# Loads, batches and splits in the setup of a four-layer kernel: the scan's weights first, up to four blocks per PSUM bank

## The reference

```
x = x + scan_attention(layernorm(x))    # attn_W, freq_W, out_W, proj_W, identity; 9 doubling steps
x = x + experts(layernorm(x))           # dense gated MLP + top-8 of 1024 experts by product keys
x = x + linear_attention(layernorm(x))  # Wq, Wk, Wv, Wo, gamma, beta
x = x + experts(layernorm(x))           # the same weights as the second layer
```

## Time and profile before

| | us |
|---|---|
| median of 3 runs | 2409.92 (2403.93 to 2412.46) |
| profiled execution | 2408.92 |
| its span | 2407.2 |
| PE busy | 2224.7 (92%) |
| DVE busy | 1902.4 (79%) |
| ACT busy | 1127.6 (47%) |
| POOL busy | 80.9 (3%) |
| mean granted clock of PE | 0.987 |

### The profile page before, as it was taken

One profiled execution on the slowest core, in us unless ns is written; L12 is line 12 of the kernel. 1 busy time (PEld: TensorE's weight loads), 2 busy tenths in 40 slices (PEclk: granted clock), 3 DMA queues, 4 the chain that ended last, 5 costly groups with the idle time before them and its releaser, 6 DMA issues. The chain is left out here.

```text
span 2407.2 us, 37844 instructions
## 1 busy us (share of the span) xinstructions
PE 2224.7 (92%) x12582; PEld 1548.4 (64%) x12582; DVE 1902.4 (79%) x5516; ACT 1127.6 (47%) x1542; POOL 80.9 (3%) x135
## 2 busy tenths in 40 slices
PE   5999999899999999999979999988999999999998
PEld 4777777676576676676734455446576576675674
DVE  5768686689889898998965566556888889898997
ACT  1445454453543544434426666663543544444533
POOL 3200000000000000000000000000000000000000
PEclk9999999999999999999989999999999999999999
DMA  7000000000000000000000000000000000000000
GB/s 210 1 1 0 0 0 1 1 1 1 0 0 0 0 0 0 0 0 0 1 1 1 1 1 0 1 1 1 1 9 9 0 9 9 0 9 9 0 10 9
DMA packets 20761, 18.10 MB, mean 8 GB/s; under 512 B 6555, under 2 KB 19871, under 8 KB 20648
## 3 DMA queue, kind: packets, MB, share of 16 engines
q1 hardware_dynamic: 16106, 14.04, 1.9%
q10 hardware_dynamic: 4542, 2.78, 0.4%
HBM read 12.60 MB, written 4.19 MB: 7 GB/s over the span
## 5 line engine op out<-in xcount | busy, mean ns | idle before, releaser
L1380 ACT ACTIVATE f_E<-f_two 128x1024 f32<-128x1024 f32 x256 | 248.2, 1021 | 324.8 <-PE f_two L1265 324.8
L1111 DVE SCALAR_TENSOR_TENSOR f_E<-f_two,f_E 128x1024 f32<-128x1024 f32 x256 | 311.2, 1221 | 91.1 <-ACT f_E L1380 84.7
L1255 PE MATMUL f_acc<-ue,f_mid 128*128 128x256 f32 x1024 | 251.9, 392 | 6.2 <-DVE f_mid L1096 6.2
L1255 PEld LDWEIGHTS f_acc<-ue,f_mid 128*128 128x128 f32 x1024 | 191.0, 193 | 47.4 <-issue 15.4
L1163 PE MATMUL f_two<-f_hT,wg 128*128 128x512 f32 x768 | 210.3, 409 | 0.0
L1350 ACT ACTIVATE f_gate<-f_two,bg 128x512 f32<-128x512 f32 x128 | 88.1, 688 | 257.6 <-PE f_two L1163 257.3
L1163 PE MATMUL f_two<-f_hT,wu 128*128 128x512 f32 x768 | 199.9, 395 | 0.0
L1835 ACT ACTIVATE b_U<-b_two 128x768 f32<-128x768 f32 (+1 forms) x192 | 158.8, 882 | 65.5 <-PE b_two L1700 64.8
L1163 PE MATMUL f_two<-f_hT,deT 128*128 128x512 f32 x768 | 184.3, 395 | 0.0
L1591 DVE TENSOR_TENSOR b_U<-b_U,tri 128x512 f32<-128x512 f32 x128 | 85.4, 689 | 116.3 <-ACT b_U L1835 116.3
L1163 PEld LDWEIGHTS f_two<-f_hT,wu 128*128 128x128 f32 x768 | 144.2, 188 | 35.0
(11 more groups left out here) (262 smaller groups left out, 3950.7 us busy)
## 6 DMA issues: line engine op xcount, KB each, us to landing
x<-in_L_attn_a_x SPq DMA_DIRECT2D x8, 512.0 KB, 7.5
out_x<-x SPq DMA_DIRECT2D x8, 512.0 KB, 2.9
de_rows<-in_L_ffn_down_embed ACTq DMA_DIRECT2D x1, 1024.0 KB, 6.0
wd<-in_L_ffn_Wd SPq DMA_DIRECT2D x1, 1024.0 KB, 10.1
ue<-in_L_ffn_up_embed SPq DMA_DIRECT2D x16, 64.0 KB, 5.2
whole_g<-in_L_ffn_Wg SPq DMA_DIRECT2D x1, 1024.0 KB, 5.4
whole_u<-in_L_ffn_Wu SPq DMA_DIRECT2D x1, 1024.0 KB, 8.7
ffq<-in_L_ffn_Wq ACTq DMA_DIRECT2D x4, 128.0 KB, 8.9
```

What stands on the lines that cost most here:

```text
L1111: dve.scalar_tensor_tensor(out=two_heads, in0=wide(turns, ("R", u))[:], scalar=PICKED_ABOVE, in1=two_heads, op0=ALU.is_gt, op1=ALU.mult).t ...
L1255: mm = pe.matmul(acc[:, j * C:(j + 1) * C], mixed[c % 2][:, j * P:(j + 1) * P], w.ue[:, c, :], start=False, stop=True, skip_group_check=True)
L1380: act.activation(E[:, c % 2, 2 * p:2 * p + 2].rearrange("p h t -> p (h t)"), wide(turns, ("S", u))[:], ACT.Exp).then_inc(S.act_read, 1)
```

## The change

The nine scan loads are issued ahead of x(0) and x(1). ACT issues its ten loads only when all nine scan loads have landed. SP issues x(2) and all later loads only when ACT's loads and the columns have landed.

A job now holds a list of pieces, each a turn or a product, side by side in one bank: up to four transposes of 128 columns, or four products of 64. TensorE signals after the last piece, and VectorE copies the whole bank with one instruction. The number of transposes and products is as before. The scan's jobs become 4 turns and 12 products, keys and ffq 3 jobs, wsim 4, de 4, wrow 6.

VectorE takes the statistics and moments of x(0) ahead of jobs 6 and 7 and those of x(1) ahead of jobs 8 and 9, and normalises four tiles behind the second wsim job and four behind the fourth. The third subtraction (second half of `deT`) moves from GpSimd to the end of VectorE's list.

```diff
@@ -176,55 +176,59 @@
 
         jobs = []
 
-        def turned(src, dst):
-            jobs.append(([(src, None)], P, dst, 1.0))
+        def turned(srcs, dst):
+            jobs.append(([[(src, None)] for src in srcs], P, dst, 1.0))
+
+        def product(pairs, m, dst, scale):
+            jobs.append(([pairs], m, dst, scale))
 
         for k in range(KC):
-            turned(outw[:, k * P:(k + 1) * P], outwT[:, k, :])
-            for r in range(KC):
-                turned(attnw[:, r, k * P:(k + 1) * P], attnqT[:, k, r * P:(r + 1) * P])
+            cols = slice(k * P, (k + 1) * P)
+            turned([outw[:, cols]], outwT[:, k, :])
+            turned([attnw[:, r, cols] for r in range(KC)], attnqT[:, k, :])
 
         for half in range(2):
...
         scan_jobs = len(jobs)
+        turned([keys[:, k, :] for k in range(KC)], keysT[:])
         for k in range(KC):
-            turned(keys[:, k, :], keysT[:, k, :])
-            for h in range(H):
-                turned(ffq[:, k, h].rearrange("p q n -> p (q n)"), ffqT[:, h, k * P:(k + 1) * P])
-        for q in range(2):
-            for h in range(H):
+            turned([ffq[:, k, h].rearrange("p q n -> p (q n)") for h in range(H)], ffqT[:, :, k * P:(k + 1) * P])
+        for k in range(KC):
+            for q in range(2):
                 rows = slice(q * NKEYS, (q + 1) * NKEYS)
-                for k in range(KC):
-                    jobs.append(([(ffqT[rows, h, k * P:(k + 1) * P],
-                                   keysT[rows, h // 2, (h % 2) * NKEYS:(h % 2 + 1) * NKEYS])],
-                                 P, wsim[:, k, (q * H + h) * NKEYS:(q * H + h + 1) * NKEYS], 1.0))
+                jobs.append(([[(ffqT[rows, h, k * P:(k + 1) * P],
+                                keysT[rows, h // 2, (h % 2) * NKEYS:(h % 2 + 1) * NKEYS])] for h in range(H)],
+                             P, wsim[:, k, q * C:(q + 1) * C], 1.0))
         wsim_made = len(jobs)
         deT_made = []
         for k in range(KC):
-            for e in range(FC):
-                block = deT[:, k].rearrange("p (q i l) -> p i q l", q=LQ, l=NHI)[:, 2 * e:2 * e + 2]
-                turned(de[:, e, k * P:(k + 1) * P], block)
+            for e in range(0, FC, 4):
+                block = deT[:, k].rearrange("p (q i l) -> p i q l", q=LQ, l=NHI)[:, 2 * e:2 * e + 8]
+                turned([de[:, e + n, k * P:(k + 1) * P] for n in range(4)], block)
             deT_made.append(len(jobs))
         for k in range(KC):
-            for r in range(2):
-                turned(wrow[:, 0, r, k * P:(k + 1) * P], w.wqk[:, k, r * P:(r + 1) * P])
-                turned(wrow[:, 1, r, k * P:(k + 1) * P], w.wqk[:, k, C + r * P:C + (r + 1) * P])
-                turned(wrow[:, 2, r, k * P:(k + 1) * P], w.wvb[:, k, r * P:(r + 1) * P])
-                turned(wrow[:, 3, r, k * P:(k + 1) * P], w.wo[:, k, r * P:(r + 1) * P])
+            cols = slice(k * P, (k + 1) * P)
+            turned([wrow[:, m, r, cols] for m in range(2) for r in range(2)], w.wqk[:, k, :])
+            turned([wrow[:, 2, r, cols] for r in range(2)], w.wvb[:, k, :])
+            turned([wrow[:, 3, r, cols] for r in range(2)], w.wo[:, k, :])
+
+        def job_bank(n, pieces, m):
+
+            width = P if pieces[0][0][1] is None else pieces[0][0][1].shape[-1]
+            return bank[n % 4][0:m, 0:width * len(pieces)], width
+
         splits = [(w.wsim[:, 0], w.wsim[:, 1], wsim, wsim_made)]
         for k in range(KC):
             splits.append((w.deT[:, 0, k], w.deT[:, 1, k], deT[:, k], deT_made[k]))
@@ -241,16 +245,17 @@
                     sp.dma_start(w.x[:, b * TJ:(b + 1) * TJ, :],
                                  io.x[b].rearrange("(j p) c -> p j c", p=P)).then_inc(w.x_loaded[b], 16)
 
+                for dst, src in scan_loads:
+                    sp.dma_start(dst, src, allow_slow_non_contiguous=True).then_inc(scan_loaded, 16)
                 load_x(0)
                 load_x(1)
-                for dst, src in scan_loads:
-                    sp.dma_start(dst, src, allow_slow_non_contiguous=True).then_inc(scan_loaded, 16)
                 for signal in w.all_signals:
                     sp.sem_inc(signal, START)
                 sp.sem_inc(signals_open, 1)
                 sp.wait_ge(features_cleared, 1)
                 for dst, src in columns:
                     sp.dma_start(dst, src, allow_slow_non_contiguous=True).then_inc(loaded, 16)
+                sp.wait_ge(loaded, 16 * (len(loads) + len(columns)))
                 for b in range(2, B):
                     load_x(b)
                 sp.dma_start(w.wd[:], io.Wd.rearrange("(f p) n -> p f n", p=P)).then_inc(w.ue_loaded, 16)
@@ -305,7 +310,7 @@
                 pool.wait_ge(signals_open, 1)
                 scan_deviations(pool, w, 0)
 
-                for n, (upper, lower, whole, _) in enumerate(splits):
+                for n, (upper, lower, whole, _) in enumerate(splits[:2]):
                     pool.wait_ge(upper_made, n + 1)
                     pool.tensor_tensor(lower, whole, upper.bitcast(F32), ALU.subtract)
 
@@ -313,25 +318,29 @@
             def _(pe):
                 pe.wait_ge(scan_loaded, 16 * len(scan_loads))
                 pe.wait_ge(ident_ready, 1)
-                for n, (products, m, dst, scale) in enumerate(jobs):
+                for n, (pieces, m, dst, scale) in enumerate(jobs):
                     if n == scan_jobs:
                         pe.wait_ge(loaded, 16 * (len(loads) + len(columns)))
                     if n >= 4:
                         pe.wait_ge(job_out, n - 3)
-                    width = products[0][1].shape[-1] if products[0][1] is not None else P
-                    out = bank[n % 4][0:m, 0:width]
-                    if products[0][1] is None:
-                        pe.transpose(out, products[0][0], w.ident[:]).then_inc(job_done, 1)
+                    out, width = job_bank(n, pieces, m)
+                    if pieces[0][0][1] is None:
+                        for c, [(src, _)] in enumerate(pieces):
+                            mm = pe.transpose(out[:, c * P:(c + 1) * P], src, w.ident[:])
+                        mm.then_inc(job_done, 1)
                         turned_last = n
                         continue
                     if n == turned_last + 1:
                         pe.wait_ge(job_out, n)
-                    for k, (lhsT, rhs) in enumerate(products):
-                        mm = pe.matmul(out, lhsT, rhs, start=(k == 0), stop=(k == len(products) - 1))
+                    for c, products in enumerate(pieces):
+                        for k, (lhsT, rhs) in enumerate(products):
+                            mm = pe.matmul(out[:, c * width:(c + 1) * width], lhsT, rhs,
+                                           start=(k == 0), stop=(k == len(products) - 1))
                     mm.then_inc(job_done, 1)
 
             @block.scalar
             def _(act):
+                act.wait_ge(scan_loaded, 16 * len(scan_loads))
                 for dst, src in loads:
                     act.dma_start(dst, src, allow_slow_non_contiguous=True).then_inc(loaded, 16)
                 act.wait_ge(steps, 4 + 2 * H)
@@ -372,26 +381,37 @@
                                   ALU.mult, ALU.add).then_inc(chain, 1)
                 dve.wait_ge(chain, 2)
                 split_biases(slice(0, NGIVEN), 0)
-                dve.wait_ge(signals_open, 1)
-                for b in range(2):
-                    dve.wait_ge(w.x_loaded[b], 16)
-                scan_stats(dve, w, 0, range(2 * TJ))
-                for l in range(2):
-                    scan_moments(dve, w, 0, l)
-                for n, (products, m, dst, scale) in enumerate(jobs):
+                for n, (pieces, m, dst, scale) in enumerate(jobs):
+                    if n == 6:
+                        dve.wait_ge(signals_open, 1)
+                        dve.wait_ge(w.x_loaded[0], 16)
+                        scan_stats(dve, w, 0, range(0, TJ))
+                    if n == 7:
+                        scan_moments(dve, w, 0, 0)
+                    if n == 8:
+                        dve.wait_ge(w.x_loaded[1], 16)
+                        scan_stats(dve, w, 0, range(TJ, 2 * TJ))
+                    if n == 9:
+                        scan_moments(dve, w, 0, 1)
                     if n == scan_jobs:
                         dve.wait_ge(job_out, n)
                         split_biases(slice(NGIVEN, NBIAS), 1)
-                        scan_normalise(dve, w, 0)
-                    width = products[0][1].shape[-1] if products[0][1] is not None else P
+                    out, _ = job_bank(n, pieces, m)
                     dve.wait_ge(job_done, n + 1)
-                    src = bank[n % 4][0:m, 0:width]
                     if len(dst.shape) == 4:
-                        src = src.rearrange("p (i q l) -> p i q l", q=LQ, l=NHI)
+                        out = out.rearrange("p (i q l) -> p i q l", q=LQ, l=NHI)
+                    elif len(dst.shape) == 3:
```

(11 more changed lines are left out.)

10 lines of the change are left out of this document (4 added, 6 removed).

## The result

| | before | after |
|---|---|---|
| median, same chip | 2408.46 us | 2400.32 us |
| range of the 7 runs | 2403.93 to 2412.46 | 2398.91 to 2404.54 |
| profiled span | 2407.2 | 2398.6 |
| first instruction of the scan | 54.72 | 44.53 |

The ratio is 0.9965, 95% interval 0.9955 to 0.9976: 8.1 us less by the medians. The interval leaves out 1, so the kernel is faster, by well under 1%. 2397 had been forecast. The scan starts 10.2 us earlier; 12.7 had been forecast.

What follows compares the result with a forecast made beforehand. The setup ahead of the scan was taken as the bound of the gain, with VectorE's chain deciding: scan start 54.7 - 42.0 = 12.7 us less, 2409.9 - 12.7 = 2397.2, forecast 2397, range 2392 to 2405.

Steps and rivals of the forecast that it cites:

- `loaded`: Semaphore for ACT's loads and the columns: complete at 22.4, bounds 20.5 and 25.7; columns land by about 22.
- The scan's loads: SP's nine first loads: wv issued by 7.65, weights there at about 9.3 instead of 20.6, signals open at 15.05.
- old pace: Rival: SP's backlog of issues keeps its pace, scan starts at 46.2 or 44.0, 8.5 us less, 2401.5; chance 0.14.
- VectorE's chain: VectorE's setup work, expected to decide: second bias split done at 24.6, three copies at 26.4, everything at 41.4.
- TensorE's part: Setup behind keys and ffq: 16 products in 6.3 us, 32 transposes in 3.48 + 3.44 us; nothing shrinks.
- cheap copies: Rival: VectorE's fixed cost per copy was on the setup's path, another 3.8 us, 2393.5; chance 0.09.
- What holds the end: End of setup: SP's last 25 loads take 17.96 us behind `loaded`, ending at 40.4, 1.0 us ahead of VectorE's 41.4.
- SP ends last: Rival: `loaded` at 23.5 to 26, setup ends 18.3 later, 42 to 44.3, 2397 to 2400; chance 0.68 together with forecast.
- The third subtraction: On VectorE behind its last copy: 1.22 us, ending at 41.4; this tail stays the same size.
- The time: Whole kernel: 12.7 us less than the median 2409.9, forecast 2397, range 2392 to 2405; chance of faster 0.86.
- One sign of being wrong: Stages behind the scan's first instruction: taking over 3 us more or less than before would show the prediction wrong.

## Why the prediction was right, point by point

Both parts of the change shortened the setup, together by 10.2 us, and the time fell into the range. The path that ends the setup was not the one I expected, though, and that the forecast came within 3.3 us owes something to luck: `loaded` came 3.5 us late, the products ran 1.6 us faster than I had it, and SP's list was nearly as long as VectorE's.

- **The scan's loads.** Right, and better than the value taken: issue ran at 0.47 us each, the lower bound, with wv issued at 6.76 (7.65 forecast) and the signals open at 14.25 (15.05). The rival "old pace" is refuted. TensorE's start was at 10.89, later than the 9.3 I had for the bytes (the terms given for it, 3.9 and 4.9, add to 8.8).
- **`loaded`.** The term that was off most: 25.9 where 22.4 was forecast, just outside the bound of 25.7. I gave the columns 1.6 us to land, as on idle engines, and said that taking turns would spare them a queue behind ACT's bulk. They landed in 3.7 to 6.5 us, and one gamma's issue took 3.59. The bulk was in at 23.8; the last column set `loaded`, 2.1 us later. The Trainium skill's rule (DMA: Bandwidth & Descriptors, Queues, rings and completion order) was read one-sidedly: if the engines take turns packet by packet, the two thousand 4-byte pieces of bg and bu get as many turns as the bulk's pieces. The trace agrees for them: from 17 to 20 q1 moved 2051 packets and q10 1679, and the stretch at 18 to 19 moved 121 GB/s. It does not explain the eight later columns, gamma and beta with 16 elements each: they took 4.3 and 4.2 us in the median, and the last, issued by 22.2, landed at 25.9. Why they took so long beside the bulk, instead of 1.6, is open. With the columns gone, `loaded` came at 22.5 in two kernels, at 22.9 and 23.3 in two executions of a third, and at 24.2 and 24.3 in two more.
- **VectorE's chain.** It ended at 41.88 (41.4 forecast), right by errors that cancel. It resumed behind `loaded` at 26.67 instead of 24.6, and the 16 products took 4.67 us instead of 6.3. The prediction said that nothing of TensorE's part shrinks; that step was wrong. It also had TensorE set the pace to the end. From 33.73 to 41.88 the rows of VectorE follow one another without a gap, with four normalisations (1.38 us) among them, while TensorE's last transpose was done at 39.65. So the end of the chain was VectorE's own work. The 0.217 us per transpose that stood against "cheap copies" is TensorE's pace at its lower clock; at the higher one 16 transposes took 2.36 us, 0.15 each.
- **What holds the end.** I had SP 1.0 us ahead of VectorE; it came 2.2 us behind, since its 18.2 us (17.96 forecast) hang on `loaded` alone, with nothing to make up the delay. The prediction expected VectorE to decide, and that was wrong; the rival "SP ends last", which it had counted in with the forecast, gave 44.3 for a `loaded` of 26. Shown by taking SP's loads out, by taking the wait out, and by lengthening SP's list.
- **The third subtraction.** 1.22 us behind VectorE's last copy, as forecast; worth 0.4 by the estimate above.
- **Cheap copies.** Refuted as to its size here: de's and wrow's transposes and copies took 6.92 us (33.82 to 40.74), 0.4 less than before and not 3.8.
- **The time.** The setup gave 10.2 us, the medians 8.1, the interval 5.8 to 10.8. The executions' own later stages vary by more than the difference of 2. The forecast time of 2397 was 3.3 us too low and inside its range of 2392 to 2405, which was wide enough for this path or VectorE's; of the forecast 12.7 us two thirds came. One sign of being wrong was set too tight: stages behind the setup over 3 us longer or shorter than before, where two executions of the changed kernel gave 1.6 and 4.1.

## What to carry to other kernels

When a stage ends at a barrier, an engine that only issues DMAs is a path like any other: if its list hangs on a late semaphore, loads that nobody needs yet belong behind the barrier. Keep loads in pieces of 4 bytes out of the semaphore of a wait if nobody behind it reads them: beside a bulk load they land late (3.7 to 6.5 us against 1.5 to 2.6). But then look where they go, since behind x(7) they lengthened the list that held the barrier. Read a setup's gain from the start of the next stage, since the later stages of one kernel alone can vary by as much as the gain.

## What the runs showed of the hardware that I had not expected

- Products on partitions 0 to 63 and on 64 to 127, in neighbouring jobs and different banks, overlap: 16 of them took 4.67 us when the half changed three times, 6.26 with one change, and 6.35 before, also with one.
- Small pieces keep the DMA engines busy and move little: in the slowest microsecond with Wq's 256-byte pieces they moved 140 to 232 GB/s, and with the columns' 4-byte pieces beside those 69 to 127. The 1 KB pieces alone moved 323 at 22 to 23.
- The landing of the same loads moved by up to 1.8 us between executions that issue them alike (22.5 to 24.3), and with it the whole setup. Two of these kernels (`loaded` at 22.5 and 24.2) differ only in jobs behind `loaded`, so the kernel's text does not explain it.
- TensorE did most of this setup at the lower level of its clock, and its mean granted clock does not tell so: 16 transposes took 3.67 us, the next 16 in the same kernel 2.36.
